# Causal attention: each chunk's attend moved directly behind the next chunk's scores

## What is computed

```python
Q = einsum('bsd,hdk->bhsk', x, Wq) * m
K = einsum('bsd,hdk->bhsk', kv, Wk) * m
V = einsum('bsd,hdk->bhsk', kv, Wv) * m
energy = einsum('bhsk,bhtk->bhst', Q, K)
lengths = sum(energy[:, :, 0, :] != 0, axis=-1)
energy = where(cols >= lengths, -inf, energy)
energy = where(cols[None, :] > cols[:, None], -inf, energy)
score = softmax(energy / sqrt(dk), axis=-1)
out = einsum('bhst,bhtk->bhsk', score, V) * m
```

## Time and profile before

| | us |
|---|---|
| median of 3 runs | 2807.34 (2805.86 to 2809.14) |
| the profiled execution, its span | 2805.9 |
| PE busy in it | 2723.5 (97%) |
| DVE, ACT, POOL busy | 1882.0, 1634.7, 637.8 |
| causal phase, first to last scores | 1408.5 to 1956.5 |
| one turn of the loop, on PE | 34.4 |

### The profile page before, as it was taken

How to read it: one execution, slowest core, us unless ns; L and a number is a source line. 1 busy time by engine, 2 the same in 40 slices (tenths; PEclk the granted TensorE clock), 3 DMA queues, 4 the chain that set the end, 5 groups by cost and what they waited for, 6 DMA issues and landing times.

```text
span 2805.9 us, 68735 instructions
## 1 busy us (share of the span) xinstructions
PE 2723.5 (97%) x24272; PEld 2360.1 (84%) x24272; DVE 1882.0 (67%) x5544; ACT 1634.7 (58%) x4949; POOL 637.8 (23%) x755
## 2 busy tenths in 40 slices
PE   6999999999999999999999999999999999999997
PEld 5888888887888888888888888888888888888886
DVE  6778778777544443445377777777677767767766
ACT  6878877888211111111277777777666666656664
POOL 1111111111000000000023333333233424324333
PEclk9999999999999999999999999999999999999999
DMA  3333332333302112012021111113111111101100
GB/s 119 108 99 99 106 112 86 106 107 99 124 30 60 45 45 60 30 60 88 33 83 51 47 45 45 45 45 105 36 45 37 37 45 45 39 36 45 45 30 24
DMA packets 145494, 178.45 MB, mean 64 GB/s; under 512 B 16272, under 2 KB 75664, under 8 KB 144912
## 3 DMA queue, kind: packets, MB, share of 16 engines
q1 hardware_dynamic: 145424, 177.53, 19.7%
HBM read 121.92 MB, written 55.57 MB: 63 GB/s over the span
## 4 chain that ended last, share of the span: by engine, by line
PE 40%; DVE 5%; issue 2%; ACT 2%; POOL 1%; POOLq 0%; DVEq 0%; ACTq 0%
PE cross_work L172 15%; PE causal_work L172 7%; PE cross_probsT L1961 2%; PE cross_attended L1980 2%; PE cross_scores L1940 2%; PE cross_scores L1961 2%; PE causal_attended L1980 1%; PE causal_scores L1961 1%; PE causal_scores L1940 1%; PE causal_probsT L1961 1%; PE cross_scores L1889 1%; DVE causal_scores L1323 1%; POOL causal_y L610 1%; PE causal_probsT L1922 1%; PE cross_probsT L1922 1%
## 5 line engine op out<-in xcount | busy, mean ns | idle before, releaser
L2804 ACT ACTIVATE mlp_h<-mlp_f,mlp_b1col 128x512 f32<-128x512 f32 x128 | 88.3, 690 | 526.7 <-PE mlp_f L3002 526.7
L3002 PE MATMUL mlp_f<-mlp_xT_hi,mlp_w 128*128 128x512 f32 x1024 | 335.1, 389 | 0.0
L3020 PE MATMUL mlp_acc<-mlp_w,mlp_hT_hi 128*128 128x512 f32 x1024 | 315.2, 389 | 0.0
L2905 DVE CAST mlp_hT_hi<-mlp_h 128x512 fp32r<-128x512 f32 x128 | 57.7, 451 | 375.3 <-ACT mlp_h L2804 375.2
L790 ACT ACTIVATE mask_prob<-mask_scores,mask_low 128x256 f32<-128x256 f32 x512 | 237.1, 475 | 21.5 <-DVE mask_low L1323 21.2
L790 ACT ACTIVATE cross_prob<-cross_scores,cross_low 128x256 f32<-128x256 f32 x512 | 237.5, 499 | 7.2 <-DVE cross_low L1317 7.0
L1323 DVE CUSTOM_DVE_ANT_0 mask_scores<-mask_scores,mask_mask 128x256 f32<-128x256 f32 x512 | 201.4, 457 | 46.4 <-PE mask_scores L1940 46.4
L172 PE MATMUL causal_work<-causal_xT_hi,causal_w 128*128 128x256 f32 x1008 | 227.6, 297 | 0.5
L3020 PEld LDWEIGHTS mlp_acc<-mlp_w,mlp_hT_hi 128*128 128x128 f32 x1024 | 192.3, 188 | 40.0
L3002 PEld LDWEIGHTS mlp_f<-mlp_xT_hi,mlp_w 128*128 128x128 f32 x1024 | 192.3, 188 | 39.8
L790 ACT ACTIVATE causal_prob<-causal_scores,causal_low 128x128 f32<-128x128 f32 (+1 forms) x512 | 211.3, 436 | 19.6 <-DVE causal_low L1323 19.6
(11 more groups left out here) (339 smaller groups left out, 8254.1 us busy)
## 6 DMA issues: line engine op xcount, KB each, us to landing
cross_x_in<-after_attention SPq DMA_DIRECT2D x17, 512.0 KB, 3.7
mask_x_in<-in_x SPq DMA_DIRECT2D x16, 512.0 KB, 4.7
mask_c_in<-in_ctx SPq DMA_DIRECT2D x16, 512.0 KB, 5.6
mask_res<-in_x SPq DMA_DIRECT2D x16, 512.0 KB, 3.6
after_attention<-mask_res SPq DMA_DIRECT2D x16, 512.0 KB, 2.8
mlp_x<-after_attention SPq DMA_DIRECT2D x8, 1024.0 KB, 5.6
mlp_stage<-in_L_xattn_fc_w SPq DMA_DIRECT2D x8, 1024.0 KB, 5.6
after_layer<-mlp_y SPq DMA_DIRECT2D x8, 1024.0 KB, 4.3
```

The lines of the kernel that those rows point to most:

```text
L2804: act.activation(h32[:, m % 2, :], F1[m % 2][:], ACT.Gelu, bias=b1col[:, m:m + 1]).then_inc(s["gelu"], 1)
L3002: ins = pe.matmul(F1[m % 2][:], W[2 * (m // 4)][:, a, k, m % 4 * P:(m % 4 + 1) * P], xT[p][:, k, :], start=(k == 0 and n == 0), stop=(k == ...
L3020: ins = pe.matmul(ACC[t][:], hT[a][:, m % 2, t * P:(t + 1) * P], W[2 * (m // 4) + 1][:, p, m % 4, :], start=(m == 0 and n == 0), stop=(m = ...
```

## The change

On PE, a chunk's order was: scores of this chunk, transposes of the last chunk's last head, half or all of a values' product, attend of the last chunk, and so on. Now it is: transposes of the last chunk's last head, scores of this chunk, attend of the last chunk; the values' product stands ahead of those transposes, behind the third head's. In the loop body each of the four chunks has this form. ACT's order follows: `values(b, 0)` is taken at the head of the turn, `copy(b, 2)` stands ahead of `qk(b, 2)`, `copy(b, 6)` and `copy(b, 7)` each stand ahead of one of the two `turned`. On DVE the second `turned(b + 1, 1)` moves from ahead of `minima(b, 2)` to between its second and its third head.

PE, from here on chunks 0 to 2 of the loop body as it is now:

```diff
+            if prev:
+                turn_probs(b, -1)
             if cur:
                 scores(b, 0)
...
+                attend(b, -1)
...
+            queries(b, 2)
+            turn_probs(b, 0)
+            energies0(b, 1)
+            keys(b, 2, 0)
+            turn_probs(b, 1)
+            if prev:
+                attended(b, -1)
+            keys(b, 2, 1)
+            pe.wait_ge(s["len_ready"], KC * b + 2)
+            turn_probs(b, 2)
+            pe.wait_ge(s["v_ready"], 2 * b + 1)
+            values(b, 1, 0)
+            turn_probs(b, 3)
+
+            scores(b, 1)
+            attend(b, 0)
...
+            queries(b, 3)
+            turn_probs(b, 4)
+            energies0(b, 2)
+            keys(b, 3, 0)
+            turn_probs(b, 5)
+            attended(b, 0)
+            keys(b, 3, 1)
+            if nxt:
+                values(b, 1, 1, 0)
...
+            turn_probs(b, 6)
+            if nxt:
+                values(b, 1, 1, 1)
...
+            turn_probs(b, 7)
+
+            scores(b, 2)
+            attend(b, 1)
...
+                queries(b + 1, 0, 0)
...
+            energies0(b, 3)
...
                 queries(b + 1, 0, 1)
...
+            turn_probs(b, 8)
+            if nxt:
+                keys(b + 1, 0)
...
+            turn_probs(b, 9)
+            attended(b, 1)
+            pe.wait_ge(s["len_ready"], KC * b + 4)
+            turn_probs(b, 10)
             if nxt:
                 values(b + 1, 0, 0)
...
+            turn_probs(b, 11)
```

DVE, in its `causal_turn`:

```diff
             if nxt:
                 turned(b + 1, 0)
-                turned(b + 1, 1)
             elif cur:
                 yield ROOM
 
             if cur:
-                minima(b, 2)
+                minima(b, 2, (0, 1))
+                if nxt:
+                    turned(b + 1, 1)
+                minima(b, 2, (2, 3))
```

ACT, in its `causal_turn` (one piece of four):

```diff
                 qk(b, 3)
+                if not nxt:
+                    yield ROOM
+                copy(b, 6)
             if nxt:
                 turned(b + 1, 0)
...
                 copy(b, 7)
                 if nxt:
-                    values(b, 1)
+                    turned(b + 1, 1)
                 exps(b, 8)
                 if not nxt:
                     yield ROOM
                 exps(b, 9)
+                if nxt:
+                    values(b, 1)
```

More of the change, by code:

```diff
@@ L931, in causal_turn @@
                 copy(b, -1)
+            if cur and prev:
+                values(b, 0)
             if not cur:
@@ L1019, in causal_turn @@
                     yield ROOM
-            if nxt:
+            if cur and nxt:
+                copy(b, 14)
                 qk(b + 1, 1)
@@ L2273, in causal_turn @@
+            turn_probs(b, 6)
+            if nxt:
+                values(b, 1, 1, 1)
             else:
                 yield ROOM
-            if prev:
-                attended(b, -1)
-            if cur:
-                keys(b, 2, 1)
-                pe.wait_ge(s["len_ready"], KC * b + 2)
-                turn_probs(b, 2)
-            if cur:
-                scores(b, 1)
-                turn_probs(b, 3)
-                values(b, 1, 1, 0 if nxt else None)
-            if cur:
-                attend(b, 0)
-                pe.wait_ge(s["qk_lo"], KC * b + 3)
-                queries(b, 3)
-                turn_probs(b, 4)
@@ L2372, in causal_turn @@
                 keys(b + 1, 1, 0)
[L2373 removed]
+            else:
                 yield ROOM
[L2375 to L2377 removed]
+            turn_probs(b, 13)
+            attended(b, 2)
             if nxt:
```

116 lines of the change are left out of this document (28 added, 88 removed).

## The result

| | before | after |
|---|---|---|
| median of 5 runs, us | 2806.96 (2805.74 to 2809.14) | 2816.94 (2814.74 to 2818.26) |
| ratio after/before | | 1.0037, 95% interval 1.0025 to 1.0049 |
| span of the profiled execution, us | 2805.9 | 2813.0 |
| turn of the causal loop (PE, scores 0 to scores 0), us | 34.38 | 35.04 |

2818.5 was predicted, slower. The profiled execution of the changed kernel is the one with the shortest time of its five (2814.74; its mean granted clock is 0.997, against 0.994 to 0.996 in the other four); hence the 7.1 us between the spans against 10.0 between the medians.

A forecast was written before the change was run, and what follows sets the result against it. PE, 97% of the span, bounds the kernel. Chunks 8.73, 8.54, 9.64 and 8.32 make 35.23 against 34.39: +0.84 times 14, +11.8; last turn -0.6, span 2817.1, median 1.4 above: 2818.5 us, range 2797 to 2825.

The forecast's parts named there:

- Attend behind scores: PE, every chunk: one change of array form fewer, the direct one taken at 0.09; chunk 8.27 against 8.43.
- Stop at the flags in chunk 0: PE: third head's transposes wait for DVE's flags, starting 6.52 to 6.60 against 6.15 planned; new stop of 0.41.
- the 0.10 that I added for a restart behind a wait: PE: a matmul row following a wait starts with its weight load, counted as starting 0.10 later.
- Attended, 0.05 in three chunks: PE, chunks 0, 1 and 3: attended, planned at 5.16, begins at 5.21 behind ACT's copy ending at 5.06.
- Chunk 1, 0.23: PE: fourth head's transposes wait for ACT's third copy, beginning 1.26 behind the third's instead of 1.03.
- The second low part: DVE, chunk 2: second xT_lo misses the border of POOL's gains and waits out the second; PE stops 1.30 per turn.
- The sum: Causal loop turn: four chunks with their stops, 35.23 against 34.39, +0.84; times 14 turns +11.8.
- The last turn: End of the causal loop: gains its four pairs, -0.6; order around the next phase's opening left at nothing, within 2 us.
- A: Rival, chunk 2: low part slips in ahead of POOL's second gain, PE stops 0.24; 2801, case called 2803; chance 0.30.
- B: Rival: direct change free, stops of chunks 0 and 1 vanish; -1.25 per turn, 2789; chance 0.14 including cases between A and B.
- C: Rival: attend waits for ACT's late copy of the fourth head, decisive above 0.3 us of lateness; 2825; chance 0.06.
- DVE's chain as unbroken: Argument against B: turn_over and flags on DVE form an unbroken chain, so the stops stay.

The follow-up runs named there:

- e5_form: Changed kernel with queries ahead of attend on PE in chunks 0 and 3, so attend no longer follows scores directly; 2819.1 us (one time).
- e2_cuts: Changed kernel with cuts(b, 1) on DVE between the two turn_overs instead of behind both; 2817.0 us.
- e11_keys: Changed kernel with the second half of keys(b, 3) on PE in chunk 1 behind the third head's transposes, no longer ahead; 2826.4 us (one time).
- e4_gain: Changed kernel with the next turn's query0 on POOL ahead of the gains instead of behind them; 2810.1 us (one time).
- e1_head: Changed kernel with the second xT_lo on DVE behind one head's masks of chunk 2 instead of two; 2806.2 us, ratio to before 0.9998.
- e9_over2: e8_over with turned(b + 1, 0) on DVE ahead of the second turn_over; 2794.4 us, 0.9957 of before.
- e6_old_dve: Changed kernel with DVE's old order: second xT_lo directly behind the first, ahead of all chunk 2 masks; 2803.2 us, ratio to before 0.9984.
- e8_over: e1_head plus ACT's values copy ahead of exps(b, 9) and DVE's second turn_over moved from chunk 0 to the end of chunk 1; 2802.3 us.

## Why the prediction was right, step by step

Direction, mechanisms and the four chunks came out as forecast. For the turn 35.23 was predicted and 35.04 measured.

- **Attend behind scores, 0.16 a chunk.** Chunk 3, which has no new stop, went from 8.42 to 8.27: 0.15. e5_form gives 0.15 for the way back.
- **Stop at the flags in chunk 0.** 0.41 predicted, transposes at 6.52 to 6.60. Measured: flags end at 6.30 (1661.61) instead of 6.36, transposes start at 6.44, stop 0.34. The transposes' own slot is 0.05 longer, and e2_cuts removed both: 0.39. What was too large is the 0.10 that I added for a restart behind a wait: of it only these 0.05 show, while behind the long wait of chunk 2 six matmuls take 0.82 instead of 0.71.
- **Attended, 0.05 in three chunks.** Nothing: ACT's copy ended at 5.06 as predicted and attended started at 5.16, its planned place. The same 0.10 was added once too often.
- **Chunk 1, 0.23.** Measured 0.13 (slot 0.92 instead of 0.79): the copy began 0.53 behind the transposes and took 0.49, as predicted, and PE started 0.15 behind its end. Again without the 0.10. That the wait is ACT's third copy is shown by the rows and by the comparison with the other chunks at e11_keys.
- **The second low part.** Predicted: border at 10.95 behind scores 1, low part issued at 11.16, end at 12.76. Measured: 10.93 to 10.97, 11.06 and 12.76. e4_gain took the gains away and left 0.69 of 1.70; e1_head changed the place and got 1.08; e9_over2 got 0.70 with the low part 0.11 ahead of the second gain. Of the terms this is the one that makes the sign: e6_old_dve, without it, is faster than before.
- **The sum.** +0.84 a turn was predicted and +0.66 measured: 0.07, 0.12 and 0.05 too much in chunks 0, 1 and 3, 0.04 too little in chunk 2 (the wait ended 0.07 sooner, the matmuls behind it took 0.11 longer; the terms listed for that chunk add up to 8.32 and not to 8.34). Against e6_old_dve, where the low part is early, the whole stop of chunk 2 is 1.40: 1.30 of waiting and 0.10 in the matmuls behind it. From turn 0 to the last turn +11.8 was predicted and +8.4 measured, of which 2.5 are those 0.18 us and 0.8 turns 0 and 1, above all the stops of turn 1 of before, which I had not looked at. The last turn was taken at -0.6 and came out at +0.2, and the cross phase at -1.4 instead of 0. On the span that makes 7.1 against 11.2. The median came within 1.6 us of the forecast, the span only within 4.1 (2813.0 against 2817.1): part of the close hit is luck, since the median stands 3.9 above the span here and not 1.4.
- **Rivals.** A (the low part slips in) was close: the low part came 0.13 us behind the border, and 0.2 was the working's; 0.13 is no more than the error of the forecast for chunk 1 alone (8.54 against 8.42), and in e8_over the order of a low part and `query0` fell both ways at 0.11 to 0.13. So the mechanism was right, but that it and not A came was won by a margin that the sum could not vouch for. In e1_head and e9_over2 the low part does slip in; e1_head then took 2806.2, not A's 2801, since ACT's copy came late. B's 2789 was not reached by any kernel; its -1.25 is the turn without any wait (33.14), which still pays for the direct change, so its sum does not hold what its words say (free, with the 0.09 of each of four chunks, it would be -1.61). C did not come: attend starts 1.12 to 1.13 behind scores in all four chunks.

What the prediction did not see is the other side: how cheaply the stops come away. I had weighed DVE's chain as unbroken, and so it is, but only between the masks of chunk 0 and those of chunk 1. At the end of chunk 1 there were 0.75 us to spare.

## What to carry to other kernels

When an instruction is moved, look at what runs on the engine that shares its memory port at the new place, and write down the distance to the nearest border of that engine's instructions: a low part 0.13 us behind the border waited for 1.0 us and stopped PE for 1.2, 14 times. Where that distance is of the size of the sum's own error, both orders have to be priced. When a stop is removed, look for the next engine in the chain before you book the gain: here DVE's low part, then ACT's copy, then DVE's masks took turns, and each needed one more moved statement. A stop that moves to the next chunk when its cause is reordered shows a chain without slack; then only moving work out of the chain helps, into an idle time that the timeline shows.

## What the runs showed of the hardware

- The exclusion works both ways, and for whole instructions. In e9_over2 the second low part was issued 0.11 ahead of the second gain, had SBUF there and ran 0.70; POOL's two gains took 3.00 instead of 2.53. In e8_over query0 of POOL took 1.15 instead of 0.71 beside the first low part. DVE's `cut` (one SBUF input, 0.35 alone) took 0.97 beside the later gains of the changed kernel. The masks, which read PSUM and one SBUF tile, kept their 0.30 and 0.47 beside them, and the transposes of turn_over (SBUF to SBUF, one input) their 1.12 beside query0.
- At a border between two gains of POOL, which follow each other without a gap, it was the waiting DVE instruction that came next, in e1_head, e8_over and e9_over2 alike. The Trainium skill, SBUF — State Buffer, section "SBUF: two separate sides", says that whichever starts first has the shared pair of ports for the whole instruction. The traces agree, with the border as the place where the order is made anew, but the recorded starts tell the order only roughly: in six turns of e8_over the low part went first with a record that begins 0.11 to 0.13 behind query0's.
- An instruction of PE that waits restarts 0.04 to 0.15 us behind the end of the instruction it waits for. Transposes behind ACT's copy of a unit: 0.14 to 0.15 (1671.82 to 1671.97; 1677.36 to 1677.50). Attended behind ACT's copy of the rows in e1_head: 0.04 to 0.05 (1674.69 to 1674.73). Behind DVE: 0.05 for the low part (1676.75 to 1676.80), 0.14 for the flags (1661.61 to 1661.75).
